# Non-local block on 16 images: order of the first three and the last two images, dummy matmuls, a split first load, and the place of the shifted scores

## What is computed

```
theta = x W_theta                       1024 pixels x 32
phi   = maxpool2x2(x W_phi)              256 cells  x 32
g     = maxpool2x2(x W_g)                256 cells  x 128
beta  = softmax(theta phi^T, over cells)
out   = gamma * (beta g) W_o + x
```

## Time and profile before

| | |
|---|---|
| median of 3 runs | 263.77 us |
| profiled execution | 264.32 us |
| its span | 262.5 us |
| TensorE matmul busy | 242.1 us (92%) |
| VectorE busy | 208.0 us (79%) |
| ScalarE busy | 148.5 us (57%) |
| GpSimd busy | 167.2 us (64%) |
| chain that ended last, on TensorE | 79% |
| mean DMA rate | 195 GB/s |

### The profile page before, as it was taken

One profiled execution on the slowest core, in us unless ns is written; L12 is line 12 of the kernel. 1 busy time (PEld: TensorE's weight loads), 2 busy tenths in 40 slices (PEclk: granted clock), 3 DMA queues, 4 the chain that ended last, 5 costly groups with the idle time before them and its releaser, 6 DMA issues.

```text
span 262.5 us, 4313 instructions
## 1 busy us (share of the span) xinstructions
PE 242.1 (92%) x1456; PEld 211.7 (81%) x1456; DVE 208.0 (79%) x475; ACT 148.5 (57%) x274; POOL 167.2 (64%) x117
## 2 busy tenths in 40 slices
PE   0869499999999999999999999999999999999973
PEld 0658378889898989888898989898888989897862
DVE  4746638798897979797988979797979989798743
ACT  4253557483838566574838385665749384727240
POOL 1362747676786958676767869586757778535270
PEclk9998959999999999999999999999999999999998
DMA  7700080482919385674929193855739292808354
GB/s 261 278 0 0 1 302 21 140 345 87 345 57 332 144 262 223 185 298 115 366 82 355 64 330 139 263 219 182 299 118 366 81 326 103 295 3 310 132 202 161
DMA packets 14646, 51.14 MB, mean 195 GB/s; under 512 B 1824, under 2 KB 2208, under 8 KB 14624
## 3 DMA queue, kind: packets, MB, share of 16 engines
q1 hardware_dynamic: 14624, 50.86, 54.2%
HBM read 33.95 MB, written 16.78 MB: 193 GB/s over the span
## 4 chain that ended last, share of the span: by engine, by line
PE 79%; DVE 9%; DMA 3%; issue 3%; ACT 2%; POOL 1%; SPq 1%; DVEq 0%; ACTq 0%
PE proj L160 31%; PE out L249 25%; PE shift L249 8%; PE shift L226 6%; PE score L190 5%; PE score L212 4%; DVE neg_parts L427 3%; DVE y_sb L453 2%; DMA x_t<-in_xt 2%; DVE g_max L420 2%; DMA theta<-neg_lo 2%; DVE out L402 1%; DVE theta L408 1%; POOL x_lo L363 1%; PE score L199 1%
## 5 line engine op out<-in xcount | busy, mean ns | idle before, releaser
L368 POOL TENSOR_TENSOR e_lo<-e_sb,e_hi 128x512 fp32r<-128x512 f32 x64 | 81.8, 1291 | 58.3 <-ACT e_sb L327 58.3
L363 POOL TENSOR_TENSOR x_lo<-x_t,x_hi 128x1024 fp32r<-128x1024 f32 x31 | 74.2, 2393 | 25.3 <-ACT x_hi L286 25.3
L160 PE MATMUL proj<-x_hi,w_hi 128*128 128x512 f32 x128 | 53.6, 419 | 7.2 <-DVE x_lo L467 6.3
L249 PE MATMUL out<-G_hi,e_hi 128*128 128x258 f32 x192 | 57.4, 299 | 2.3 <-issue 1.4
L249 PE MATMUL out<-G_lo,e_hi 128*128 128x258 f32 x192 | 54.4, 283 | 0.0
L249 PE MATMUL out<-G_hi,e_lo 128*128 128x258 f32 x192 | 54.2, 282 | 0.0
L160 PE MATMUL proj<-x_hi,w_lo 128*128 128x512 f32 x128 | 53.0, 414 | 0.0
L160 PE MATMUL proj<-x_lo,w_hi 128*128 128x512 f32 x128 | 52.8, 412 | 0.0
L324 ACT ACTIVATE e_hi<-shift 128x512 fp32r<-128x512 f32 x64 | 38.5, 602 | 24.7 <-PE shift L226 24.7
L453 DVE SCALAR_TENSOR_TENSOR y_sb<-out,r_sum,x_n 128x256 f32<-128x256 f32 x96 | 46.4, 484 | 7.3 <-DVE r_sum L444 1.0
L427 DVE TENSOR_REDUCE neg_parts<-score 128x2 f32<-128x512 f32 x64 | 43.7, 686 | 0.9
(11 more groups left out here) (49 smaller groups left out, 362.5 us busy)
## 6 DMA issues: line engine op xcount, KB each, us to landing
x_t<-in_xt SPq DMA_DIRECT2D x32, 512.0 KB, 4.4
x_n<-in_xn SPq DMA_DIRECT2D x32, 512.0 KB, 7.0
out<-y_sb SPq DMA_DIRECT2D x32, 512.0 KB, 6.2
w_sb<-in_w_proj SPq DMA_DIRECT2D x1, 256.0 KB, 2.7
theta<-neg_hi SPq DMA_DIRECT2D x16, 4.0 KB
theta<-neg_lo SPq DMA_DIRECT2D x16, 4.0 KB
wo_sb<-in_w_out SPq DMA_DIRECT2D x1, 128.5 KB, 4.5
```

The source lines that it names most:

```text
L160: last = nc.tensor.matmul(proj[h][:, :], w[:, c, cols:cols + P], x[:, i % 2, h, c, :], start=(c == 0 and n == 0), stop=(c == CC - 1 and n ...
L249: last = nc.tensor.matmul(out_bank(t)[:, 0:GW], e[:, i % 2, KC * h + k, cells], G[:, i % 3, k, :], start=(n == 0), stop=(n == 3 * KC - 1))
L363: nc.gpsimd.tensor_tensor(x_lo[:, i % 2, h], x_t[:, i % 2, h], x_hi[:, i % 2, h].bitcast(f32), ALU.subtract).then_inc(x_lo_ready, 1)
L368: nc.gpsimd.tensor_tensor(e_lo[:, i % 2, n, :], e_sb[:, n, :], e_hi[:, i % 2, n, :].bitcast(f32), ALU.subtract).then_inc(e_lo_ready, 1)
```

## The change

- **Loads.** Half 0 of image 0 comes as two transfers of 256 KB, one per channel block, issued by ScalarE on its own queue with semaphores `x0_in`. SyncE issues weights, half 1 of image 0, W_o, images 1, 2 and (behind the first x_n) 3.
- **Dummy matmuls.** TensorE begins with 8 matmuls of 512 columns on a part of e_lo that GpSimd has set to zero, into `score[0]`.
- **First images.** The stages 0, 1 and the projections and scores of stage 2 are written out on each engine. Values of image 0 go to the `shift` banks; mixes of images 0 and 1 go to `outb[0]`; mix of image 0 comes behind its scores. The first projection runs in another order of its six products. wo_hi moves to ScalarE, wo_lo to GpSimd.
- **Every stage.** `shifted(b, 0)` and `shifted(b, 1)` stand ahead of output 6 instead of behind it. On VectorE `G_low` stands behind `finish` of tile 5 instead of tile 4. Outputs 0 and 4 wait for each part of e and e_lo just ahead of the matmul that reads it.
- **Last images.** In stage 15 two scores of image 15 stand where the mix was; the mix goes to `proj[0]` behind output 7; the rest is written out, with four banks in turn for the outputs of image 15. The last half is stored as three transfers (tiles 0 and 1, tile 2 from ScalarE's queue, tile 3).

```diff
-        G_bank, neg_bank = score
+        neg_bank = score[1]
...
+        def value_bank(i, h):
+            return shift[h] if i == 0 else proj[h]
+
+        def mix_bank(i):
+            return outb[0] if i < 2 else proj[0] if i == LAST else score[0]
+
+        def out_bank(i, t):
+            if i == LAST:
+                return (outb[0], outb[1], shift[0], shift[1])[t % 4]
             return shift[t - 2] if t in (2, 3) else outb[t % 2]
...
             def output(i, t):
                 h, w = divmod(t, HT)
                 if t == 0:
-                    pe.wait_ge(G_lo_ready, i + 1)
-                if w == 0:
-                    pe.wait_ge(e_lo_ready, 4 * i + KC * h + KC)
+                    pe.wait_ge(G_lo_ready, max(i + 1, 2))
...
+                    if w == 0:
+                        pe.wait_ge(e_ready, 4 * i + KC * h + k + 1)
                     for e, G in ((e_hi, G_hi), (e_hi, G_lo), (e_lo, G_hi)):
+                        if w == 0 and e is e_lo:
+                            pe.wait_ge(e_lo_ready, 4 * i + KC * h + k + 1)
...
+            pe.wait_ge(warm_ready, 1)
+            for n in range(WARM):
+                nc.tensor.matmul(score[0][:, :], e_lo[:, 1, 3, 0:P], e_lo[:, 1, 3, :], start=True, stop=True)
+
+            first_project()
+            values(0, 0)
+            theta_phi(0, 1)
+            values(0, 1)
+
+            theta_phi(1, 0)
+            scores(0, 0)
+            scores(0, 1)
+            theta_phi(1, 1)
+            scores(0, 2)
+            scores(0, 3)
+            values(1, 0)
+            turn_max(0)
+            mix(0)
+            values(1, 1)
+
+            theta_phi(2, 0)
+            shifted(0, 0)
+            scores(1, 0)
+            shifted(0, 1)
+            theta_phi(2, 1)
+            mix(1)
+            scores(1, 1)
+            shifted(0, 2)
+            values(2, 0)
+            scores(1, 2)
+            shifted(0, 3)
+            values(2, 1)
+            scores(1, 3)
...
+                if a < LAST:
+                    outputs(d, (0, 1, 2))
+                    turn_max(b)
+                    outputs(d, (3, 4))
+                    mix(a)
+                    output(d, 5)
+                else:
+                    outputs(d, (0, 1, 2))
+                    turn_max(b)
+                    output(d, 3)
+                    scores(a, 0)
+                    output(d, 4)
+                    scores(a, 1)
+                    output(d, 5)
+                shifted(b, 0)
+                shifted(b, 1)
+                outputs(d, (6, 7))
+
+            mix(LAST)
+            scores(LAST, 2)
+            shifted(LAST - 1, 2)
+            scores(LAST, 3)
+            shifted(LAST - 1, 3)
+            outputs(LAST - 1, (0, 1))
+            turn_max(LAST)
+            outputs(LAST - 1, (2, 3, 4, 5))
+            shifted(LAST, 0)
+            shifted(LAST, 1)
+            outputs(LAST - 1, (6, 7))
+            shifted(LAST, 2)
+            shifted(LAST, 3)
+            outputs(LAST, range(TILES))
...
+            for c in range(CC):
+                act.dma_start(x_t[:, 0, 0, c, :], xt[0, 0, :, c, :]).then_inc(x0_in[c], 16)
             first_x_high(0)
             first_x_high(1)
             x_high(0, 1)
...
+            nc.gpsimd.memset(e_lo[:, 1, 3, :].bitcast(f32), 0.0).then_inc(warm_ready, 1)
```

VectorE's list for the first three images, and SyncE's for the last:

```diff
+            phi_pool(0, 0)
+            theta_low(0, 0)
+            g_pool(0, 0)
+            phi_pool(0, 1)
+            theta_low(0, 1)
+            phi_low(0)
+            g_pool(0, 1)
+            maxima(0, 0)
+            maxima(0, 1)
+            phi_pool(1, 0)
+            theta_low(1, 0)
+            maxima(0, 2)
+            maxima(0, 3)
+            phi_pool(1, 1)
+            neg_low(0)
+            theta_low(1, 1)
+            phi_low(1)
+            g_pool(1, 0)
+            G_low(0)
+            g_pool(1, 1)
+
+            phi_pool(2, 0)
+            theta_low(2, 0)
+            maxima(1, 0)
+            phi_pool(2, 1)
+            theta_low(2, 1)
+            G_low(1)
+            phi_low(2)
+            maxima(1, 1)
+            g_pool(2, 0)
+            maxima(1, 2)
+            g_pool(2, 1)
+            maxima(1, 3)
...
+            store(LAST, 0)
+            sp.wait_ge(y_ready, TILES * LAST + 6)
+            sp.dma_start(out[LAST, 1, :, 0:2, :], y_sb[:, 1, 0:2, :]).then_inc(y_out[1], 16)
+            sp.wait_ge(y_ready, TILES * LAST + 8)
+            sp.dma_start(out[LAST, 1, :, 3:4, :], y_sb[:, 1, 3:4, :]).then_inc(y_out[1], 16)
```

More of the change, by code:

```diff
@@ L97, in loads, with loads_t @@
             return 16 * (i // 2 + 1)
+        def loads_t(i, h):
+            return loads(i) - 16 if i % 2 == 0 and h == 0 else loads(i)
         def neg_loads(i):
@@ L153, in _, with first_project @@
+            sp.wait_ge(y_ready, TILES * LAST + 8)
+            sp.dma_start(out[LAST, 1, :, 3:4, :], y_sb[:, 1, 3:4, :]).then_inc(y_out[1], 16)
+            sp.wait_ge(y_out[0], 16 * B)
+            sp.wait_ge(y_out[1], 16 * (B + 2))
         @block.tensor
         def _(pe):
-            def project(i, h, cols, done):
+            def first_project():
+                for n, c in ((0, 0), (1, 0), (0, 1), (1, 1), (2, 0), (2, 1)):
+                    if n == 0:
+                        pe.wait_ge(x0_hi_ready, c + 1)
+                        pe.wait_ge(w_hi_ready, 1)
+                    elif n == 1:
+                        pe.wait_ge(w_lo_ready, 1)
+                    else:
+                        pe.wait_ge(x0_lo_ready, c + 1)
+                    w, x = ((w_hi, x_hi), (w_lo, x_hi), (w_hi, x_lo))[n]
+                    last = nc.tensor.matmul(proj[0][:, :], w[:, c, 0:P], x[:, 0, 0, c, :],
+                                            start=(n == 0 and c == 0), stop=(n == 2 and c == 1))
+                last.then_inc(tp_ready, 1)
@@ L252, in output, with outputs @@
                 last.then_inc(out_ready, 1)
-            pe.wait_ge(fixed_ready, 4)
-            for s in range(B + 2):
+            def outputs(i, ts):
+                for t in ts:
+                    output(i, t)
+            pe.wait_ge(warm_ready, 1)
[5 more added lines that the diff above has]
+            values(0, 1)
@@ L266, in _ @@
                         values(a, h)
-                    if real(b):
                         scores(b, 2 + h)
[L269 to L278, removed]
+                if a < LAST:
[4 more added lines that the diff above has]
+                    output(d, 5)
+                else:
+                    outputs(d, (0, 1, 2))
[5 more added lines that the diff above has]
+                    output(d, 5)
@@ new lines, in _ @@
+                neg_low(b)
+                if a < LAST:
+                    finishes(d, (3, 4, 5))
+                    G_low(a)
+                    finishes(d, (6, 7))
+                else:
+                    finishes(d, (3, 4))
+                    maxima(a, 0)
+                    finishes(d, (5,))
+                    maxima(a, 1)
+                    finishes(d, (6, 7))
+            G_low(LAST)
+            maxima(LAST, 2)
+            maxima(LAST, 3)
+            finishes(LAST - 1, (0, 1))
@@ L502 @@
+            neg_low(LAST)
+            finishes(LAST - 1, range(2, TILES))
+            finishes(LAST, range(TILES))
 _INS = ["x", "L0_conv_W_theta", "L0_conv_W_phi", "L0_conv_W_g", "L0_conv_W_o", "L0_conv_gamma"]
```

227 lines of the change are left out of this document (135 added, 92 removed).

## The result

The changed kernel took 256.84 us (median; 256.68 to 257.59 in four runs), 0.973 of the kernel before, with an interval of 0.969 to 0.978: faster, by 2.7%. Forecast were 255.8 us and a range of 250.0 to 260.5. The kernel before was run again beside each set of experiments, with medians of 264.44, 264.07 and 264.10 us. One early execution of it took 467.44 us; it is left out of the ratio.

A forecast was written before the change was run, and what follows sets the result against it. Bounds: twelve steady stages of 14.46 us with TensorE almost never idle, between an opening and a tail largely spent waiting. Sum: 264.3 - 11.0 (opening) + 5.7 (stages) - 3.2 (tail) = 255.8 us, range 250.0 to 260.5.

The forecast's parts named there:

- The wait of the shifted scores: Steady stages 3 to 14: shifted scores ahead of output 6 wait for neg_lo's transfer, +0.43 us a stage, +5.7 in all.
- x: Steady stage: time from issue of neg_lo's transfer to first shifted matmul, taken as 1.85 us, bounds 1.80 and 2.15.
- The late landing: Steady stages: one transfer of neg_lo landing late as in the kernel before, 0.5 us within the +5.7.
- The opening: Start up to image 3: reordered first images shorten it from 51.3 to 40.3 us, -11.0, bounds -13 and -7.5.
- The scaling of W_o: Opening: could meet GpSimd's x_lo of half 1 and hold VectorE up to 2.4 us, changing the sum at most 0.6.
- G_low's place: Steady stages: G_low behind the finish of tile 5 costs nothing, or its 0.69 us if its cover went.
- The tail: From image 15's projections to the end: 37.7 us becomes 34.5 through less idle time, -3.2, bounds -5 and -1.
- the ending: End of the tail: 3.07 us becomes 2.4 with 128 KB instead of 512 KB stored last, bounds 1.8 and 3.1.
- the one that ended at 259 for a late landing in all stages: Rival, steady stages: every transfer lands late, 12 x 0.73 = 8.8 us, total 259.2; chance 0.17.
- the slower one: Rival, steady stages: the transfer's completion falls among x_t load packets; at x = 3.0 the total is 270.2; chance 0.04.
- the one with an opening that wins only 7.5: Rival, opening: handovers, half clock after idle and useless dummies limit the gain to 7.5 us, total 259.3; chance 0.18.
- a free move of the shifted scores: Rival, steady stages: the shifted scores never wait, saving 12 x 0.26 us, total 246.3; chance 0.09.

## Why the prediction was right, and where it was off

**The wait of the shifted scores: right in kind and size.** The step said that the transfer could not have landed by the end of output 5 and that each stage would cost x - 1.42, with x taken as 1.85. Measured are x = 1.80 and 14.81 against 14.44, +0.37, where 1.80 gives +0.38. It had been the lower bound, seen in a single quiet landing. The packets' places were a weak reason for taking it as the typical one, since in the late landing they lie in the same place; that it came out so is in part luck. Undoing (-0.47 with G_low's 0.11 in it), doing it alone (+0.37), and doing more of it (+1.04) agree. The Trainium skill's 2.0 us fixed per DMA (DMA: Bandwidth & Descriptors, "Anatomy of one DMA"), which the page gives for GpSimd's path, would have put the stage at 15.06, an estimate; the measured 1.76 decides. (The total of 257.5 that the prediction made from it left out the 0.5 for a late landing.)

**The late landing: mis-sized.** 0.5 was set aside for one. It cost 1.19 (a stage of 16.00), and in other profiles with a late landing 0.2 to 3.1. With 12 x 0.37 + 1.19 = 5.6 the term still came out near its +5.7, because x was smaller; by the stage starts it is 5.40, as the kernel before has its own late landing inside.

**The opening: right sum, in good part by cancelling.** The chain began 1.05 later (10.85 instead of 9.8 for theta/phi of half 1) and ran faster (0.23 a matmul, where 0.38 was assumed; in the profile without dummies it was 0.43 here until 12.61), so that its twelve matmuls were over 0.6 early. The step then allowed theta/phi of image 1 only 0.9, though no row shows six such matmuls in under 1.39; they took 1.40 and ended at 15.3, which was the forecast. VectorE's row maxima ended within 0.1 of the forecast by two more errors that cancel: 16.3 us of work instead of 17.2, and 2.8 of waits instead of 2.0 (columns as in the earlier trace rows, the third busy time is VectorE's):

```profile
14.55:33.61 19.06, 16.76 (x91) 14.07 (x90) 16.34 (x27) 13.13 (x25) 12.85 (x10) 1.00 0.23 89
```

That the idle time ahead of 22.55 would cost half pace was wrong in this execution: the matmuls behind its 1.66 us follow at 0.23, and the 0.5 set aside for it was not needed. In its place GpSimd, not VectorE, set a wait of 0.70 before the mix of image 2, which no step had. The scaling of W_o, which the prediction feared would meet GpSimd's x_lo, ran ahead of it (at 8.01, for 0.35). Which of the many edits brings how much of the 10.86 was not tried, but for the dummies and the split load; the experiments show only that these two can't be the most of it.

**G_low's place: "costs nothing" was right, but it wins 0.11** a stage in the order of before, since output 7 no longer waits for y of tile 5.

**The tail: right sign, gain too large by 2.** The step gave the transfer of image 15 a wait of 0.9 for standing behind the loads of x_n. It was 2.2: 3.95 us to land, while the DMA engines were still busy with these loads and the store behind them. The stretch of the changed kernel while it is on its way and the one in which it has landed (us, then busy time of PE, PEld, DVE, ACT and POOL, the granted clock, DMA share, GB/s):

```profile
238.90:242.40 3.50, 1.78 (x15) 1.56 (x13) 2.27 (x8) 0.00 (x0) 0.16 (x1) 1.00 0.80 295
242.40:242.90 0.50, 0.03 (x1) 0.03 (x1) 0.00 (x0) 0.00 (x0) 0.00 (x0) 1.00 0.06 25
```

Three kernels that took it out from behind the loads brought it down to 1.8 to 2.04. The exps and e_lo of image 15 cost 1.3, near the 1.4 of the forecast: between the shifted scores at 242.87 and output 0's last wait, which ends at 247.15, lie 4.3 us, of which two outputs of image 14, four shifted matmuls and the first five matmuls of output 0 fill 3.0.

```profile
245.86 0.29 PE L301 MATMUL out<-G_hi,e_hi 128*128 128x258 f32 x1
...
247.15 0.39 PE L301 MATMUL out<-G_hi,e_lo 128*128 128x258 f32 x1 [0.51 <-POOL e_lo L506]
...
252.87 0.48 DVE y_sb L603
```

The other part of the miss is a term that the sum lacked. It put the ending (2.45 measured, 253.35 to 255.8, against 2.4) right behind TensorE's work, but TensorE's last matmul starts at 252.34 and the last y ends at 253.35: 0.9 us in which VectorE finishes what TensorE has done. The waits of 0.3 and 0.4 for e_lo at output 0 of image 14 and at outputs 4 didn't occur and gave some of it back.

**The sum.** 264.32 - 10.86 + 5.40 - 1.24 = 257.6, which is the profiled 257.59. Of the rivals, the one that ended at 259 for a late landing in all stages and the slower one are refuted by the steady 1.76, the one with an opening that wins only 7.5 by the 10.86, and a free move of the shifted scores (246) by every profile. The change as a whole is a gain of 12 us at the ends with a loss of 5 in between. That the profiled total came within 1.8 of the forecast is also owed to errors of unlike sign inside the opening; the signs of all three parts and the sizes of the first two were right.

## What to carry to other kernels

Before an instruction is moved ahead of others on a busy engine, measure from the issue of what it waits for to where it would now stand. What the landing takes beyond that distance is new idle time in each stage, less the waits that the move takes away (here 0.64 less 0.26), and the chain gave nothing back. Once there is such a wait, each further piece of work that is put behind it is paid in full. Two edits took the loss back here: the old order (251.5) and the transfer's producer one step earlier on its own engine (252.1). The times don't tell which is better. A small transfer that is waited for belongs ahead of the bulk loads or on another queue than they, and putting it ahead can cost part of the gain again by making the loads late. When a change of many parts is judged by one time, take the spans of opening, stage and tail from the trace separately; here they had opposite signs.

## What was not expected of the hardware

**Some landings of a small transfer are late, and a load of instructions was on its way in each.** Eleven of the thirteen profiles show one landing of the 4 KB transfer in their steady stages that takes 2.3 to 3.4 us instead of 1.76. In the three microseconds behind the issue of each of the eleven (192.06 in the kernel before, 184.56 in the changed one) the DMA queue named "instruction", q8, moved one packet of 16 KB. The queues of the changed kernel from 184.5 to 187.6 (packets, MB, share of 16 engines):

```profile
q1 hardware_dynamic: 121, 0.37, 41.6%
q8 instruction: 1, 0.02, 2.0%
```

and in the stage before, from 169.7 to 172, where the landing took 1.75:

```profile
q1 hardware_dynamic: 55, 0.10, 24.8%
```

It isn't the packet alone. The changed kernel has two more windows with such a packet, behind 66.10 and 125.32, and landings of 1.75 and 1.76 in them. In the stages of the seven profiles whose kernels wait for every landing, 21 windows have the packet: 7 are late and 14 are not, and no window without it is late. What else must come together wasn't tried, and that the packet is the cause is not shown. A place behind output 6 makes a late landing cheap but not free: the three such kernels whose profile has one took 0.2 (the kernel before), 0.4 and 0.7 longer in that stage, against 1.2 to 3.1 where the shifted scores stand ahead of output 6 and neg_low is not early.

**The pace of TensorE in an opening is not the same in each execution.** With the same 8 dummies (1.31 to 5.1 us) the first values projection ran at 0.23 or at 0.43 us a matmul, in ten profiles, and the start of image 3 moved by 1.7 us with it. The profile's granted clock tells only some of these apart. Half pace reads 1.00 where TensorE had not yet run at full pace in that execution, as without dummies (8.30 to 12.60) or in the kernel before (10.80 to 15.45, 0.43 a matmul). It reads 0.50 where the pace had been full and fell back, as in the kernel with the maxima ahead of the loads:

```profile
8.30:12.60 4.30, 4.30 (x11) 3.30 (x10) 2.01 (x3) 2.87 (x4) 3.95 (x2) 1.00 0.69 209
...
8.60:11.20 2.60, 2.60 (x7) 1.99 (x6) 1.40 (x2) 2.42 (x4) 2.60 (x2) 0.50 0.63 216
```

The first row is of the kernel without dummies, the second of the other; in both the matmuls are 0.43 apart. In an opening the distance between matmuls is what tells the pace.
